# Batch 0's context transposed on TensorE, loads in order of need on one queue, LN statistics by bn_stats, queries of the other rows in step 4

## What is computed

```
x = x + tanh(g_xattn) * attention(layernorm(x), ctx)      # 16 heads of 8, softmax over 1500 rows
x = x + tanh(g_ffn)   * ffn(layernorm(x))

attention: q = x Wq' + bq;  k = ctx Wk' + bk;  v = ctx Wv' + bv;  softmax(q k' / sqrt(8)) v;  Wo, bo
ffn:       p = sigmoid(x R' + bias); top 8 of 160 experts, normalised, times 2.5
           sum over experts of  w * down(silu(gate(x))), plus a shared expert
layernorm(x) = (x - mean) / sqrt(var + 1e-5)
```

## Time and profile before

| | us |
|---|---|
| median of 3 runs | 1145.37 (1144.56 to 1149.62) |
| the profiled execution | 1148.09 |
| its span, first to last instruction | 1146.6 |
| busy in it: PE, DVE, ACT, POOL | 1068.3, 970.7, 853.4, 597.1 |

### The profile page before, as it was taken

How to read it: one execution, slowest core, us unless ns; L and a number is a source line. 1 busy time by engine, 2 the same in 40 slices (tenths; PEclk the granted TensorE clock), 3 DMA queues, 4 the chain that set the end, 5 groups by cost and what they waited for, 6 DMA issues and landing times.

```text
span 1146.6 us, 37955 instructions
## 1 busy us (share of the span) xinstructions
PE 1068.3 (93%) x12090; PEld 707.9 (62%) x12090; DVE 970.7 (85%) x1674; ACT 853.4 (74%) x1825; POOL 597.1 (52%) x1011
## 2 busy tenths in 40 slices
PE   3698899999999999999999997779999999999998
PEld 1366677777677777777777775644555555555554
DVE  4767788888788888888888888658999999999998
ACT  3465677777777777767777776657888888888887
POOL 5797888888888888888888883000000000000000
PEclk9789999999999999999999999979999999999999
DMA  7876867777677687577676642146776777677773
GB/s 154 154 160 159 188 141 189 154 159 169 147 162 174 140 185 161 142 173 157 166 167 139 159 113 60 20 132 189 234 237 224 233 233 228 223 240 231 226 235 118
DMA packets 201815, 197.05 MB, mean 172 GB/s; under 512 B 161999, under 2 KB 168207, under 8 KB 201782
## 3 DMA queue, kind: packets, MB, share of 16 engines
q1 hardware_dynamic: 188292, 174.14, 59.5%
q0 software_dynamic: 11520, 20.99, 6.6%
q10 hardware_dynamic: 1970, 1.49, 0.6%
HBM read 109.96 MB, written 12.55 MB: 107 GB/s over the span
## 4 chain that ended last, share of the span: by engine, by line
PE 52%; DVE 13%; POOL 13%; issue 12%; SPq 5%; DMA 2%; ACT 1%; POOLq 1%; DVEq 0%; ACTq 0%
PE bank L1313 15%; PE bank L1285 15%; PE bank L1120 6%; DVE part_max L879 6%; PE bank L1134 5%; PE bank L1153 5%; DVE rec L980 3%; PE bank L1189 2%; POOL ctx_parts L492 2%; PE bank L1177 2%; POOL q_st L572 2%; POOL q_blk L556 2%; POOL w_in L465 1%; POOL w_in L467 1%; SPq L384 1%
## 5 line engine op out<-in xcount | busy, mean ns | idle before, releaser
L670 ACT ACTIVATE p_exp<-bank 125x448 f32<-125x448 f32 x768 | 400.3, 544 | 195.2 <-PE bank L1134 193.9
L879 DVE TENSOR_REDUCE part_max<-bank 128x1 f32<-128x500 f32 x672 | 420.7, 672 | 78.7 <-PE bank L1153 78.0
L1134 PE MATMUL bank<-q_st,k_stk 97*125 97x224 f16 x1536 | 276.0, 264 | 15.4 <-DMA q_st<-neg_row 8.6
L1153 PE MATMUL bank<-kparts,q_blk 128*128 128x500 f16 x672 | 256.4, 385 | 19.5 <-DVE part_max L879 16.5
L1134 PEld LDWEIGHTS bank<-q_st,k_stk 97*125 97x125 f16 x1536 | 197.2, 139 | 81.0 <-ACT p_exp L670 18.4
L1313 PE MATMUL bank<-ctT,w_ring 128*128 128x448 f16 x960 | 234.0, 353 | 3.0 <-DVE ctT L1022 3.0
L760 ACT ACTIVATE ctT<-bank 128x448 f32<-128x448 f32 x320 | 173.7, 543 | 40.4 <-PE bank L1285 15.9
L1022 DVE TENSOR_TENSOR ctT<-k_stk,ctT 128x448 f16<-128x448 f32 x320 | 198.0, 619 | 0.3 <-ACT ctT L766 0.2
L1120 PE MATMUL bank<-p_exp,v_sb 125*25 125x168 f32 (+1 forms) x6144 | 188.3, 264 | 0.6 <-ACT p_exp L670 0.6
L766 ACT ACTIVATE ctT<-k_stk 128x448 f16<-128x448 f32 x320 | 181.8, 568 | 3.5 <-DVE k_stk L1016 3.4
L1285 PE MATMUL bank<-q_hi,w_ring 128*128 128x448 f16 x640 | 174.1, 354 | 2.4 <-ACT k_stk L748 2.4
(11 more groups left out here) (149 smaller groups left out, 1231.6 us busy)
## 6 DMA issues: line engine op xcount, KB each, us to landing
v_sb<-c_scratch SPq DMA_DIRECT2D x114, 448.0 KB, 3.9
k_stk<-kparts SPq DMA_DIRECT2D x384, 93.8 KB
ctx_in<-in_ctx_dram SPq DMA_DIRECT2D x30, 672.0 KB
k_stk<-c_scratch SPq DMA_DIRECT2D x38, 448.0 KB, 3.9
w_scratch<-w_out POOLq DMA_DIRECT2D x80, 128.0 KB, 3.5
w_in<-in_L_ffn_w_gate_dram POOLq DMA_DIRECT2D x160, 32.0 KB, 3.2
w_in<-in_L_ffn_w_down_dram POOLq DMA_DIRECT2D x80, 64.0 KB, 3.5
ctx_in<-in_ctx_dram SPq DMA_DIRECT2D x30, 78.0 KB
```

The lines of the kernel that those rows point to most:

```text
L670: act.activation(p_exp[0:KP, j % PR, f * 448:(f + 1) * 448], ST[f][0:KP, 0:448], ACT.Exp).then_inc(exp_done, 1)
L879: v.reduce_max(part_max[:, i // NCH, i % NCH:i % NCH + 1], SM[i % NSM][:, 0:CK], axis=AX.X).then_inc(sm_maxed, 1)
L1134: last = pe.matmul(ST[f][0:KP, (g % 2) * GC:(g % 2 + 1) * GC], k_stk[0:97, u, g, j * KP:(j + 1) * KP], q_st[0:97, u, g, :, :].rearrange("p ...
L1153: pe.matmul(SM[i % NSM][:, 0:CK], rows, kparts[:, u, 0, c * CK:(c + 1) * CK], start=True, stop=True).then_inc(sm_done, 1)
```

## The change

- Loads: SP's queue carries x of FIRST, the four weights, the three chunks of batch 0, the context of batch 1, in this order, then the small inputs and the rows of ones. x of REST goes out on SP ahead of step 1. ScalarE's queue keeps padding and biases.
- Batch 0's context: TensorE transposes its 12 tiles in fp32 through the identity into banks 4 to 6, ScalarE copies the high part to `ctT`, VectorE subtracts for the low part. GpSimd's splits, and the DMA transposes, begin with batch 1; all their counts go down by one batch.
- LayerNorm of the attention: per group bn_stats and bn_aggr on VectorE, root on ScalarE, and x * rstd + shift in one operation, straight from xt. For REST: statistics at (1, 10) to (2, 1), spreads at (2, 1), root at (2, 2), reciprocal and shift at (2, 3), scaling on ScalarE at (3, 6), (3, 8), (3, 10).
- Queries: the 12 stacking DMAs of chunk 0 move from SP to ScalarE, behind the last of batch 0's keys. The other chunks' token transposes are at (4, 0), (4, 4), (4, 8), their products and evacuations at (4, 1), (4, 5), (4, 9), in the bank of the keys (KB); the key products of step 4 wait for `q_lo`. Their 12 stacking DMAs all go out in step 5, ahead of its row; GpSimd waits for them ahead of step 6.
- Written-out steps: 1 to 5 instead of 1 to 3 (PRO = 6); the loop starts at step 6.
- The output constant is added to FIRST ahead of step 3 and to REST ahead of step 5.
- The first keys go to banks 2, 3 and 7.

```diff
+    PRO = 6
+    STATS_REST_AT = {(1, 10): (4, 7), (1, 11): (7, 10), (2, 0): (10, 13), (2, 1): (13, 16)}
+    VAR_REST_AT, ROOT_REST_AT, RSTD_REST_AT = (2, 1), (2, 2), (2, 3)
+    SCALE_REST_AT = {(3, 6): 1, (3, 8): 2, (3, 10): 3}
+    TOKENS_REST_AT = {(4, 0): 1, (4, 4): 2, (4, 8): 3}
+    QUERIES_REST_AT = {(4, 1): 1, (4, 5): 2, (4, 9): 3}
...
-        FKB = [KB, SM[2], SM[1]]
+        FKB = SM
+        CB = [OB, KB, VB]
...
-        REST_ROWS_AT = {2: (0, 1), 3: (2,)}
-        QB = [bank[0], bank[0], bank[1], bank[0]]
+        REST_ROWS_AT = {5: (0, 1, 2)}
+        QB = [bank[0], KB, KB, KB]
...
             load_x(sp, *FIRST, x_in)
-            load_chunk(0)
             for n, w in enumerate((Wq, Wk, Wv, Wo)):
                 sp.dma_start(w_raw[:, n, :], w).then_inc(weights_in, 16)
-            for c in range(1, NCH):
+            for c in range(NCH):
                 load_chunk(c)
+            load_rows(sp, ctx_here[1], ctx_in[0:KP, 1, :, :], ctx[1].rearrange("(p j) c -> p j c", j=KT))
...
+            def rest_rows(parts):
+
+                sp.wait_ge(q_hi_done, NTC)
+                sp.wait_ge(q_lo_done, NTC)
                 for r in parts:
-                    if r == 1:
-                        sp.wait_ge(q_lo_done, c1)
                     part = (q_hi, q_lo, q_hi)[r]
                     for g in range(HG):
-                        sp.dma_start(q_stk[32 * r:32 * r + 32, g, cols], part[32 * g:32 * g + 32, cols])\
-                          .then_inc(here, 16)
+                        sp.dma_start(q_stk[32 * r:32 * r + 32, g, TC:N], part[32 * g:32 * g + 32, TC:N])\
+                          .then_inc(q_rest_rows, 16)
...
-            for c in range(NCH):
-                transpose_ctx(0, c, c + 1, None)
             small_inputs()
...
-            attention(sp, body, B - 2, {1: first_queries, 3: lambda: output_rows(0, H // 2),
+            def rest_inputs():
+                load_x(sp, *REST, x_rest)
+
+            attention(sp, body, B - 2, {1: rest_inputs, 3: lambda: output_rows(0, H // 2),
...
-            pool.wait_ge(pad_here, 32)
-            for c in range(NCH):
-                split_ctx((0, 0), c)
...
-            attention(pool, body, B - 2, {2: first_pairs, 3: add_constant, 4: all_rows})
+            attention(pool, body, B - 2, {2: first_pairs, 3: lambda: add_constant(*FIRST, 1), 5: lambda: add_constant(*REST, 4),
+                                          PRO: all_rows})
...
+            def first_context(c):
+                act.wait_ge(ct_tr, c + 1)
+                act.activation(ctT[:, 0, c, 0, :, 0:KP], CB[c][:, 0:TPC * KP].rearrange("p (j n) -> p j n", j=TPC), ACT.Copy)\
+                   .then_inc(ct_hi, 1)
+
+            def stack_first():
+
+                act.wait_ge(q_hi_done, 1)
+                act.wait_ge(q_lo_done, 1)
+                for r, part in enumerate((q_hi, q_lo, q_hi)):
+                    for g in range(HG):
+                        act.dma_start(q_stk[32 * r:32 * r + 32, g, 0:TC], part[32 * g:32 * g + 32, 0:TC])\
+                           .then_inc(q_rows, 16)
+
+            def scale_rest(t):
+                act.wait_ge(rstd_made, 2)
+                for p in range(t * PPC, (t + 1) * PPC):
+                    last = act.activation(xc[:, p, :], xt[:, p, :], ACT.Identity, scale=rstd[:, p:p + 1], bias=shift[:, p:p + 1])
                 last.then_inc(ln_done, 1)
...
+            def moments(p0, p1):
+                for p in range(p0, p1):
+                    v.bn_stats(bst[:, p, :], xt[:, p, :]).then_inc(bn_made, 1)
+
+            def spreads(p0, p1):
+
+                for p in range(p0, p1):
+                    dve.wait_ge(bn_made, p + 1)
+                    v.bn_aggr(mv[:, p, :], bst[:, p, :]).then_inc(mv_made, 1)
+                dve.wait_ge(mv_made, p1)
+                v.tensor_scalar(stat[:, 2, p0:p1], mv[:, p0:p1, 1], EPS_LN, None, ALU.add).then_inc(ln_var, 1)
+
+            def first_context(c):
+                dve.wait_ge(ct_hi, c + 1)
+                v.tensor_tensor(ctT[:, 0, c, 1, :, 0:KP], CB[c][:, 0:TPC * KP].rearrange("p (j n) -> p j n", j=TPC),
+                                ctT[:, 0, c, 0, :, 0:KP], ALU.subtract).then_inc(ct_lo, 1)
...
+            def first_context(c):
+                pe.wait_ge(first_here[c], CTX)
+                for i in range(TPC):
+                    last = pe.transpose(CB[c][:, i * KP:(i + 1) * KP], ctx_in[0:KP, 0, c * TPC + i, :], ident[0:KP, 0:KP])
+                last.then_inc(ct_tr, 1)
...
-                        pe.wait_ge(t_here[c], b * 16 + 16)
+                        pe.wait_ge(t_here[c], b * 16)
+                        if isinstance(step[0], int) and num(step) == 4:
+                            pe.wait_ge(q_lo_done, c + 2)
```

More of the change, by code:

```diff
@@ L251, in attention @@
         def attention(eng, body, loop_to=B, before={}, first=0):
-            for s in range(first, 4):
+            for s in range(first, PRO):
                 if s in before:
@@ L256, in attention @@
                 body((s // 2, s % 2))
-            if 4 in before:
-                before[4]()
-            with eng.Fori(2, loop_to // 2) as h:
+            if PRO in before:
+                before[PRO]()
+            with eng.Fori(PRO // 2, loop_to // 2) as h:
                 body((h, 0))
@@ L367, in load_ctx @@
                     b = num((h, u))
-                    sp.wait_ge(split_lo, (b - 1) * NCH)
+                    if isinstance(h, int) and b == 2:
+                        sp.wait_ge(ct_tr, NCH)
+                    else:
+                        sp.wait_ge(split_lo, (b - 2) * NCH)
                     load_rows(sp, ctx_here[u], ctx_in[0:KP, u, :, :],
@@ L387, in body @@
                     b, u = num(back(step, -1)), back(step, -1)[1]
-                    split = [b * NCH + (c + 1) for c in range(NCH)]
+                    split = [(b - 1) * NCH + (c + 1) for c in range(NCH)]
                     used = [(b - 2) * NCH + (c + 1) for c in range(NCH)]
@@ L395, in body @@
                 if isinstance(step[0], int) and num(step) in REST_ROWS_AT:
-                    stack_queries(1, NTC, REST_ROWS_AT[num(step)], q_rest_rows)
+                    rest_rows(REST_ROWS_AT[num(step)])
                 if on(step, 1):
@@ L483, in split_ctx @@
                 j = slice(c * TPC, (c + 1) * TPC)
-                if isinstance(h, int) and b == 0:
-                    pool.wait_ge(first_here[c], CTX)
-                elif c == 0:
+                if c == 0:
                     pool.wait_ge(ctx_here[u], h * CTX + (CTX if u else 0))
-                until(pool, t_here[c], b * 16)
-                split = b * NCH + (c + 1)
+                until(pool, t_here[c], (b - 1) * 16)
+                split = (b - 1) * NCH + (c + 1)
                 if not isinstance(split, int):
@@ L549, in _ @@
             pool.wait_ge(q_hi_done, 1)
+            pool.wait_ge(pad_here, 32)
             def body(step):
@@ L642, in _ @@
             act.activation(bqs[:, :], bqc[:, :], ACT.Copy, scale=QSCALE).then_inc(bqs_made, 1)
+            for c in range(NCH):
+                first_context(c)
             query_tokens(0, 1)
@@ L833, in first_keys, with deviations @@
                                        op0=ALU.add, op1=ALU.subtract).then_inc(k_lo_done, 1)
-            dve.wait_ge(x_in, 32)
-            centre(*FIRST)
-            variance(1, sq_first, *FIRST)
+            def moments(p0, p1):
[7 more added lines that the diff above has]
+                v.tensor_scalar(stat[:, 2, p0:p1], mv[:, p0:p1, 1], EPS_LN, None, ALU.add).then_inc(ln_var, 1)
+            def deviations(n, p0, p1):
+                dve.wait_ge(ln_root, n)
+                link(v.reciprocal(rstd[:, p0:p1], stat[:, 3, p0:p1]))
+                v.scalar_tensor_tensor(out=shift[:, p0:p1], in0=mv[:, p0:p1, 0], scalar=-1.0, in1=rstd[:, p0:p1],
+                                       op0=ALU.mult, op1=ALU.mult).then_inc(rstd_made, 1)
+            def first_context(c):
+                dve.wait_ge(ct_hi, c + 1)
+                v.tensor_tensor(ctT[:, 0, c, 1, :, 0:KP], CB[c][:, 0:TPC * KP].rearrange("p (j n) -> p j n", j=TPC),
+                                ctT[:, 0, c, 0, :, 0:KP], ALU.subtract).then_inc(ct_lo, 1)
+            dve.wait_ge(x_in, 32)
+            moments(*FIRST)
+            spreads(*FIRST)
+            deviations(1, *FIRST)
+            dve.wait_ge(rstd_made, 1)
+            for p in range(*FIRST):
+                last = v.tensor_scalar(xc[:, p, :], xt[:, p, :], rstd[:, p:p + 1], shift[:, p:p + 1], ALU.mult, ALU.add)
+            last.then_inc(ln_done, 1)
             for n, (lo, hi) in enumerate(((wk_lo, wk_hi), (wv_lo, wv_hi))):
```

127 lines of the change are left out of this document (51 added, 76 removed).

## The result

The kernel after took 1154.6 us, median of 8 executions (1147.0 to 1158.6), beside 1147.6 for before in the same session (1144.6 to 1149.8): ratio 1.006, 95% interval 1.0035 to 1.0085. In a second session it took 1149.8 (12 executions, 1144.2 to 1158.9) beside 1149.7: ratio 1.002, interval 0.9999 to 1.0041. The forecast was 1133.3. So 12 us of gain were expected and none came, and something new came that was in nobody's sum: executions of the same kernel now lie up to 15 us apart, where those of before lie within 5 to 7 us.

A forecast was written before the change was run, and what follows sets the result against it. The start decides, through SP's in-order DMA issues and GpSimd's chain: q_blk of step 6 moves from 146.98 to 134.5, less 0.3 for the first loop round. Sum 12.1 us, from the median 1145.37 to 1133.3; range 1127 to 1141.5.

The forecast's parts named there:

- The change, part by part: Start of the kernel: weights at 7, q_hi near 15.4, 5.8 us earlier than before; LN statistics cost 0.
- SP from there: SP's queue in the start: x's 688 KB add 3.4 us by bytes; batch 2's transpose at 43.4, first scores at 46.
- rival B: Start: bytes, not issues, limit it, so batch 2's transposes land 7.6 us later; total 1140.9; chance 15%.
- my sum by issues alone: SP's queue in the start: if issuing is the limit, first scores come at 43.5 us.
- the 7.6 us that I gave the move of the jobs: Start: moving 12 query jobs from SP to ScalarE is worth 7.6 us, by their issue times.
- GpSimd then hardly waits: GpSimd in step 2: hardly any wait for the DMA transpose of batch 2's first chunk, 2.94 us before.
- Steps 2 and 3: GpSimd done at 64.2 and 81.8 us; maxima at 83.1, with 1 us for ScalarE's scaling.
- Step 4: Transposes and query products add 4.3 us on TensorE; GpSimd ends at 108.4, TensorE at 108.6.
- rival E: Step 4: query products cost 3 to 5 us beyond TensorE's own time; total 1136.5 to 1138.5; chance 12%.
- Step 5: SP's transposes issued by 125.1, 12 rest rows take 7.5 us; q_blk of step 6 at 134.5, before 146.98.
- Behind it everything repeats: From q_blk of step 6 on: later steps repeat, so where that q_blk ends up is what counts.
- rival D: TensorE stays at half clock after the stop ahead of step 6; 24 us more, total 1157; chance 4%.

The follow-up runs named there:

- e15: e14 with x of the rest rows loaded at SP's step 2 instead of step 1 and its statistics later; 1139.9 us, ratio 0.9931 to before.
- e14: After with constant inside step 5, eight steps written out, rest rows behind the row of maxima, and q_st of step 4 waiting for o_nrm; 1137.1 us, ratio 0.9908.
- e12: After with one added wait: GpSimd's q_st products of step 4 wait for VectorE's o_nrm; 1147.0 us, ratio 0.9992 to before.
- e13: After with eight steps written out and rest rows behind the row of maxima, eight in step 5, four in step 6; constant left ahead of step 5; 1142.0 us.
- e2: Before with steps 4 and 5 written out as well, nothing else; 1147.1 us, ratio 0.9975 to before.
- e10: Whole kernel after with the constant on the rest rows moved inside step 5, behind its first chunk; 1147.7 us, ratio 0.9972 to before.
- e3: After with eight written-out steps, so GpSimd waits for the rest rows ahead of step 8, not 6; 1148.1 us, ratio 0.9986 to before.
- e4: After with eight written-out steps and rest rows sent four each in steps 5, 6 and 7, behind the row of maxima; 1152.4 us, ratio 1.0016 to before.
- e8: After cut off behind the attention, feed-forward half left out; executions 758.7 to 769.8 us, before with the same cut 761.2 to 764.6.
- e9: After cut off behind step 7, with the constant on the rest rows moved inside step 5, behind its first chunk; 190.7 us, 187.8 to 193.2.

## Why the prediction was wrong

**Two misses in one.** For the profiled execution the sum said 1136.0 and 1146.98 was measured, 11.0 us more; the forecast of the median, 1133.3, missed by 21.3 in the first session and by 16.5 in the second, because most executions of after are longer than the profiled ones. Following GpSimd's q_blk was the right choice: its lead at step 8 is what arrives at the end.

**"The change, part by part", loads, batch 0's context, statistics: right.** The weights were there at 5.84 (I took 7), q_hi started at 15.05 (15.4), GpSimd's chain held to q_blk of step 2 (41.20 for 43.1).

**"SP from there": mechanism half right, size off by 4 to 5.** I saw that x's 688 KB would collide with batch 2's transposes and charged 3.4 us by bytes: first scores at 46. They came at 50.66. The step that failed was to price the company by bytes alone; the row of maxima also stood behind the transposes on SP from 37.83 to 45.63. e15 took the company away and the transposes fell from 11 us in after (34.43 to 45.5) and 12.28 in e14 to 5.11. So rival B had the right place, and its reason in part: transfers in flight did limit this stretch, but by x's load. With the twelve query jobs still off SP and only x's load gone, e15 has its first scores at 43.34; my sum by issues alone had said 43.5. That speaks for the 7.6 us that I gave the move of the jobs. The rule that I weighed there (the Trainium skill, "DMA: Bandwidth & Descriptors", "Issuing engines are not separate DMA queues": issuing from several engines saves only sequencer time, usually little) says otherwise, and no run moved the twelve jobs alone, so that it isn't settled. Sentence "GpSimd then hardly waits": it waited 3.80 us at 46.70.

**"Steps 2 and 3": right for GpSimd but for the late start.** Its step 3 took 17.5 (67.74 to 85.28), as taken from before. For TensorE the term of 1 us for ScalarE's scaling was too small: from the sending of step 2's row to the next one 21.5 us passed (68.34 to 89.81), where I had 20.0.

**"Step 4": undersized by 2.4, and one term missing.** From row to row I had 25.5 (83.1 to 108.6); 27.9 was measured in undisturbed executions. That is rival E's mechanism, just under its lower end of 3. What I had not seen at all is the meeting of o_nrm with GpSimd. I priced the constant on the rest of x at 3.4 us of GpSimd's time, which was right to 0.1 us (3.46), and asked who waits for GpSimd; I did not ask which VectorE instruction runs at the moment to which it was moved. The meeting costs up to 6.9 us in the step, of which 4.4 to 7.3 are left at step 8. The executions above 1151 us go when it is made impossible (e12) and the spread comes back with it (e13); the profile of after shows an execution without it.

**"Step 5": the step that failed by most.** "The last transpose waits for GpSimd's last split ... 123.8, issued by 125.1" left out what stands ahead of the transposes on SP's queue: twelve key jobs, which wait for the keys until 121.01 and end at 129.4. So the transposes ended at 133.9 and not 125.1. Of these 8.8 us 4.5 were brought along, since q_blk of step 5 was that late already; my own rule, the last split 15.4 us into the step, held (112.87 to 128.2) and would have given 129.6. The other 4.3 are the key jobs ahead. The twelve rest rows then took 8.1 for 7.5 and reached GpSimd 2.7 later for 1.9. That makes the 10.3 that q_blk of step 6 was late: 4.5 brought along, 4.3 the order of the queue, 1.5 the rows. I had the same order in front of me in the earlier trace rows and used it in step 1, but not in step 5. With it I would also have seen the second thing: the row of maxima stands behind the twelve rest rows (ready 137.87, sent 142.14).

**"Behind it everything repeats": right for GpSimd, and so for the time.** q_blk of step 6 was 2.2 us ahead of before, that of step 8 1.6, the last one 0.3 behind. The profile still ended 1.2 ahead, since its last q_blk and last row of maxima lie 46.3 us apart and those of before 47.8; other profiles of this start have up to 49.1, so that was luck. TensorE did stand and run at half clock from 170 to 175, rival D's mechanism for 5 us and not the 20 that would turn the sign; by GpSimd's clock these two steps took 0.6 us more than in before. With rows and wait mended (e14) the whole is 11 us faster than before, where the forecast's gain was 12. But e2 had 2.6 us of that by writing out steps 4 and 5 alone, and I had put only 0.8 down for it; so at most some 8 to 9 us are the worth of the early start; steps 6 and 7, written out in e14 too, weren't measured alone. The forecast of the gain failed mainly on the order in SP's queue (x's load ahead of batch 2's transposes, the key jobs and the rest rows in step 5) and on the neighbour on VectorE.

**Not settled.** In all kernels with eight steps written out the way from the last row of maxima to the end is 430.3 to 431.7 us, against 428.0 in before and after; but e10, with six steps, has 430.0, so the eight steps needn't be the reason, and I have no experiment on it. The remaining spread of 4 to 7 us, also that of e12, and the longer executions of e15 are open too. The profiles show two places where it lies: q_blk of step 0 starts anywhere from 13.04 to 15.83 us in the profiles of this start, and the way from the last q_blk to the last row of maxima takes 46.3, 47.8 or 49.1 us.

## What to carry to other kernels

When a piece of work is moved in an in-order queue, write down the whole queue at the new place, with its waits, before pricing the piece; and price the piece's neighbours on the other engines, not only its own time. When executions of one kernel lie further apart than those of another, don't explain the median from one profile: cut the kernel short in stages and look at the distribution of each cut until the place is found, then look for an instruction whose own duration has changed. Before a stretch of lost time on one engine is counted as a loss, look at the engine that sets the pace: it may only be falling back to it. Two obstacles in one place hide each other, so a test that removes one (e3), or makes a new one as it removes the old (e4), and gains nothing proves nothing about it.

## What the runs showed of the hardware

- A VectorE product of 0.39 us with both inputs in SBUF took 5.81 and 6.00 us when GpSimd started a row of five SBUF-reading instructions 0.09 and 0.28 us behind it (e8, e13), and 1.94 and 2.09 with a row of four, 0.09 and 0.23 behind it (e10, e9). It got in between none of them. Where it started 0.45 us ahead of them, and so had ended, it took 0.39 (after). Of the single reductions from PSUM (part_max) in five profiles of after and its variants, two of them with such a meeting, none took longer than 0.68 us.
- Three DMA transposes behind the load of x's 688 KB needed 11.1 us (34.43 to 45.5, after) and 12.28 (e14), three ahead of it 5.11 (e15); from 25 to 50 us the queues moved less at the higher share (179 GB/s at 1.18) than at the lower (207 GB/s at 1.01, e15).
- Writing out two of the loop's steps gained 0.25% (e2).
